# Comparisons that also sum, and a count taken as a difference

## The reference

```python
h = relu(layernorm(x))
msgs_f = mlp2([h[src], h[dst], edge_attr], W1_f, b1_f, W2_f, b2_f)     # 192 -> 128 -> 128
agg    = segment_sum(msgs_f, dst, 100000)
msgs_r = mlp2([h[dst], h[src], edge_attr], W1_r, b1_r, W2_r, b2_r)
agg   += segment_sum(msgs_r, src, 100000)
out = x + h + mlp2([agg, h], Wn1, bn1, Wn2, bn2)                        # 192 -> 128 -> 64
```

## Time and profile before

| what | us |
|---|---|
| median of 3 runs | 1618.86 (1618.42 to 1619.26) |
| the profiled execution | 1619.61 |
| its span | 1617.8 |
| GpSimd busy | 1111.7 |
| VectorE busy | 977.1 |
| scatters, L532, x392 | 633.4 |
| counts, L991, x392 | 168.8 |
| comparisons, L979, x392 | 144.8 |

### The profile page before, as it was taken

How to read it: one execution, slowest core, us unless ns; L and a number is a source line. 1 busy time by engine, 2 the same in 40 slices (tenths; PEclk the granted TensorE clock), 3 DMA queues, 4 the chain that set the end, 5 groups by cost and what they waited for, 6 DMA issues and landing times.

```text
span 1617.8 us, 29085 instructions
## 1 busy us (share of the span) xinstructions
PE 1288.9 (80%) x7070; PEld 978.6 (60%) x7070; DVE 977.1 (60%) x2902; ACT 946.8 (59%) x2256; POOL 1111.7 (69%) x1003
## 2 busy tenths in 40 slices
PE   5899998457777787778788887777777756899998
PEld 4777776245556565656566665555556644666665
DVE  7999999436666666666666666666666641222222
ACT  5888888345555555545555555555554524677776
POOL 7888888888888888888888888888888861000000
PEclk9999999768888877877877778788887877999999
DMA  6899998435555555555555555555555547999997
GB/s 214 293 317 314 313 313 284 130 58 108 109 108 109 108 103 103 104 102 104 103 103 100 100 102 102 102 102 101 103 104 103 100 72 228 355 352 352 344 344 274
DMA packets 238374, 280.71 MB, mean 174 GB/s; under 512 B 53170, under 2 KB 155200, under 8 KB 238348
## 3 DMA queue, kind: packets, MB, share of 16 engines
q1 hardware_dynamic: 168408, 241.57, 45.0%
q0 software_dynamic: 68992, 38.59, 20.6%
q10 hardware_dynamic: 948, 0.30, 0.1%
HBM read 162.62 MB, written 117.72 MB: 173 GB/s over the span
## 4 chain that ended last, share of the span: by engine, by line
POOL 33%; issue 22%; DMA 15%; PE 4%; DVE 4%; ACT 1%; POOLq 0%; SPq 0%; another core or an unknown queue 0%; DVEq 0%; ACTq 0%
POOL table L532 27%; DMA out_x<-ncentred 12%; POOL got_odd L514 6%; DMA table<-to_send,scatter_at 2%; DVE ncentred L1137 2%; DVE same L979 1%; DMA same<-table 1%; PE bank L820 1%; PE bank L833 1%; PE bank L871 1%; PE bank L818 1%; PE bank L846 1%; PE bank L882 0%; SPq L391 0%; ACT nh L639 0%
## 5 line engine op out<-in xcount | busy, mean ns | idle before, releaser
L532 POOL DMA_INDIRECT table<-to_send,scatter_at x392 | 633.4, 1616 | 133.7 <-issue 119.2
L846 PEld LDWEIGHTS bank<-message,same 128*128 128x128 f32 x1960 | 271.1, 223 | 42.1 <-issue 39.2
L846 PE MATMUL bank<-message,same 128*128 128x128 f32 x1960 | 292.1, 314 | 2.7 <-DVE message L1010 2.7
L639 ACT ACTIVATE nh<-nx,all_sums,all_rstd 128x64 f32<-128x64 f32 x784 | 280.1, 433 | 0.0
L514 POOL DMA_INDIRECT got_even<-in_x,gather_first x196 | 212.0, 1082 | 40.4 <-issue 35.1
L775 PE MATMUL bank<-wn_h,nturned 128*128 128x256 f32 x784 | 197.4, 396 | 30.2 <-ACT nhidden L683 21.8
L514 POOL DMA_INDIRECT got_odd<-in_x,gather_at x180 | 179.9, 999 | 54.8 <-issue 54.2
L804 PE MATMUL bank<-ident,h_ends 128*128 128x128 f32 x196 | 54.1, 371 | 203.2 <-DVE h_ends L1019 200.8
L1004 DVE TENSOR_TENSOR scatter_at<-moved,ids 128x4 int32<-128x4 f32 x98 | 16.1, 165 | 303.3 <-DMA table<-to_send,scatter_at 303.3
L818 PE MATMUL bank<-turned,w_ends 128*128 128x256 f32 x392 | 167.0, 516 | 36.5 <-ACT turned_edge L609 36.5
L775 PEld LDWEIGHTS bank<-wn_h,nturned 128*128 128x128 f32 x784 | 143.7, 193 | 66.4 <-issue 37.8
(11 more groups left out here) (78 smaller groups left out, 1917.6 us busy)
## 6 DMA issues: line engine op xcount, KB each, us to landing
nx<-in_x SPq DMA_DIRECT2D x194, 256.0 KB
table<-nhidden SPq DMA_DIRECT2D x97, 512.0 KB
same<-table SPq DMA_DIRECT2D x97, 512.0 KB, 5.4
others<-numbers SPq DMA_DIRECT2D x196, 128.0 KB
out_x<-ncentred SPq DMA_DIRECT2D x97, 256.0 KB, 4.2
nx<-out_x SPq DMA_DIRECT2D x55, 256.0 KB, 4.7
out_x<-nh SPq DMA_DIRECT2D x31, 256.0 KB
table<-to_send,scatter_at POOLq DMA_INDIRECT x392
```

The costliest lines, as they stand in the source:

```text
L532: pool.indirect_dma_start(table, bass.IndirectOffsetOnAxis(ap=scatter_at[s][:, k:k + 1], axis=0), to_send[s][:, k, :], None, compute_op=AL ...
L639: last = act.activation(nh[s][:, g, :], nx[place][:, g, :], ACT.Relu, bias=all_sums[:, at, g:g + 1].rearrange("p a g -> p (a g)"), scale=a ...
L846: last = pe.matmul(bank[6 + s][:, k * M:(k + 1) * M], same[s][:, o, k * P:(k + 1) * P], message[s][:, o, :], start=(o == k), stop=(o == KB ...
```

## The change

The comparisons of L979 get a second operation, an addition, and an output `matches` with one number per partition: the sum of the results over all their columns, that is all ends of the same node in tiles 0 to o. The count of L991 reads only the end's own tile of `same` (128 columns each), with a mask `from_here` that is 1 from the end itself on, multiplies by -1 and starts from `matches`. What is left are the equal ends in front. The mask shrinks from 512 to 128 columns, and the scratch output `junk` too. No instruction changes its place on any engine; in the code after it, VectorE's lines stand one further down, and L991 keeps its number.

```diff
--- before.py
+++ after.py
@@ -129,7 +129,7 @@
 
 
         ident = sb("ident", [P, P])
-        earlier = sb("earlier", [P, KB * P])
+        from_here = sb("from_here", [P, P])
         spare = sb("spare", [P, KB])
         eps = sb("eps", [P, 1])
         w1_ends = sb("w1_ends", [P, 2, M])
@@ -175,7 +175,8 @@
         hidden = two("hidden", [2, JT * P])
         message = two("message", [KB, M])
         same = two("same", [KB, KB * P])
-        junk = two("junk", [KB, KB * P], mybir.dt.bfloat16)
+        junk = two("junk", [KB, P], mybir.dt.bfloat16)
+        matches = two("matches", [KB])
         before = two("before", [KB])
         to_spare = two("to_spare", [KB])
         moved = two("moved", [KB])
@@ -501,13 +502,12 @@
             pool.iota(spare[:, :], pattern=[[P, KB]], base=SPARE, channel_multiplier=1,
                       allow_small_or_imprecise_dtypes=True).then_inc(s_const, 1)
             pool.memset(ident[:, :], 0.0).then_inc(s_filled, 1)
-            pool.memset(earlier[:, :], 1.0).then_inc(s_filled, 1)
+            pool.memset(from_here[:, :], 1.0).then_inc(s_filled, 1)
             pool.wait_ge(s_filled, 2)
             pool.affine_select(out=ident[:, :], in_=ident[:, :], compare_op=ALU.not_equal, fill=1.0, base=0,
                                pattern=[[-1, P]], channel_multiplier=1).then_inc(s_const, 1)
-            tail = earlier[:, (KB - 1) * P:]
-            pool.affine_select(out=tail, in_=tail, compare_op=ALU.is_gt, fill=0.0, base=0,
-                               pattern=[[-1, P]], channel_multiplier=1).then_inc(s_const, 1)
+            pool.affine_select(out=from_here[:, :], in_=from_here[:, :], compare_op=ALU.is_ge, fill=0.0, base=0,
+                               pattern=[[1, P]], channel_multiplier=-1).then_inc(s_const, 1)
 
             def gather(to, numbers, landed, tiles=range(KB)):
                 for k in tiles:
@@ -976,7 +976,8 @@
                 row = others[s][:, :, :, :].rearrange("p j e q -> p (j e q)")
                 for o in range(KB):
                     w = (o + 1) * P
-                    last = dve.tensor_scalar(same[s][:, o, 0:w], row[:, 0:w], ids[s][:, o:o + 1], None, ALU.is_equal)
+                    last = dve.tensor_scalar(same[s][:, o, 0:w], row[:, 0:w], ids[s][:, o:o + 1], None, ALU.is_equal,
+                                             ALU.add, accum_out=matches[s][:, o:o + 1])
                 last.then_inc(s_same[s], 1)
 
             def variance(i, s):
@@ -987,9 +988,9 @@
 
                 dve.wait_ge(s_same[s], i + 1)
                 for k in range(KB):
-                    w = (k + 1) * P
-                    last = dve.tensor_tensor_reduce(junk[s][:, k, 0:w], same[s][:, k, 0:w], earlier[:, KB * P - w:],
-                                                    1.0, 0.0, ALU.mult, ALU.add, before[s][:, k:k + 1])
+                    last = dve.tensor_tensor_reduce(junk[s][:, k, :], same[s][:, k, k * P:(k + 1) * P], from_here[:, :],
+                                                    -1.0, matches[s][:, k:k + 1], ALU.mult, ALU.add,
+                                                    before[s][:, k:k + 1])
                 last.then_inc(s_before[s], 1)
                 dve.tensor_tensor(to_spare[s][:, :], spare[:, :], ids[s][:, :], ALU.subtract).then_inc(s_tospare[s], 1)
                 dve.wait_ge(s_before[s], i + 1)
```

## The result

The changed kernel takes 1610.4 us (median of 6 runs, 1608.65 to 1614.83) against 1619.06 (6 runs, 1618.42 to 1621.99): ratio 0.994, 95% interval 0.9929 to 0.9951. It is 9 us faster, where +2.5 was forecast; the profiled execution took 1610.51 us where 1622.1 was forecast.

A forecast was written before the change was run, and what follows sets the result against it. GpSimd's gathers and scatters were taken as the bound; first scatters giving back about 14 us and thirds taking about 19 made +3.8, taken as +2.5: 1622.1 us profiled, 1621.4 beside the median, range 1610 to 1626.

The forecast's parts named there:

- The bound, and the mechanism: GpSimd bounds; scatters starting during a two-input VectorE instruction begin late by about its rest less 0.10 or 0.13 us.
- I take 1.65, since the row of the same kind of output has it: L979: four summing comparisons priced at 1.65 us like the old counts, +0.17 us per batch on VectorE.
- the two more small operands I take at nothing, at most 0.01 us each: L991: the shortened counts' added operands priced at nothing; four counts go from 1.65 to 0.84 us.
- the sensitivity: Forecast change by added price: 0.01 us more per comparison +2.5 us, 0.015 -1, 0.03 -7; 0.01 on comparisons and counts -3.
- rival 1: Sum L1048 slips behind the third scatter's start if prices are 0.03 us or more higher: -7 to -9 us, 1611; chance 0.24.
- The same working: New durations put into 90 full batches' starts: scatter excess 0.297 us a batch against 0.256 before, +3.8 us.
- There is no reason left for the first scatter to suffer: 0: First scatter beside L979: excess falls from 0.152 us to 0, giving back about 14 us over the stage.
- is the most the change can give: All 392 scatters: VectorE's instructions cost GpSimd (1.616 - 1.552) x 392 = 25 us, the largest possible gain.
- The second scatter: Second scatter, beside L1019: mean excess over 1.553 us forecast at 0.07, against 0.078 before.
- Rival 2: L979 comparisons keep their two-column rate, first two scatters stay, L1048 ends 0.8 us earlier: -2 us, 1617; chance 0.12.
- Rival 3: Nearly all batches meet the L1048 collision at the third scatter, some also pay at the second: +9 us, 1628; chance 0.13.
- Rival 4: Two-input instructions cost scatters nothing, only two-column ones do: -14 us, 1605; chance 0.03.

The follow-up runs named there:

- counts-alone kernel: Kernel before with only the counts cut to 128 columns, start value constant 1, plain comparisons, all rows to the spare rows: 1617.87 us, ratio 0.9991.
- The kernel with the sum sooner: Changed kernel with the count's last two small instructions put behind the sum nodes + h, which starts sooner: 1633.94 us, ratio 1.0083.
- as-priced kernel: Changed kernel with comparisons against a constant, counts started from a constant, matches left out, all rows to the spare rows: 1630.67 us, ratio 1.0061.
- the control: Kernel before with counts started at 1, so every row goes to the spare rows: 1619.37 us, ratio 0.9999.

## Why the prediction was wrong

**The bound, and the mechanism: right.** GpSimd bounds the stage, VectorE's own time does not count (0.8 us a batch less is worth nothing in the counts-alone kernel), and a scatter pays for a two-input instruction that is running when it starts. The kernel with the sum sooner was forecast to 25 us by that rule alone. In the ten traces it holds for all 213 scatters that started well inside the sum.

**The step that failed** is "I take 1.65, since the row of the same kind of output has it", with "the two more small operands I take at nothing, at most 0.01 us each". I matched the comparison to the count by its output and passed over its operand: the comparison takes the node numbers as a column in SBUF, the old count took constants. That column costs 0.06 us in every instruction: 346 against 286 ns for a summing comparison, 346 against 287 for a count. In four comparisons and four counts this is 0.47 us, and the sum starts that much later, behind the third scatter instead of over it. It was there to be read in the earlier trace rows: the free comparison took 0.47 us where 512 columns, two at a time, and the fixed 0.15 of a count make 0.42. I used the 0.47 to tell the rate and let the 0.05 left over go. (No run has the comparison without a sum against a constant, so that the 0.05 is the same cost is likely, not shown.) The count, newly given a column by the diff, then got the same nothing.

**How much hung on it.** The prediction did carry the sensitivity: -7 us for 0.03 more per comparison, and rival 1 for that case, at 1611. It was given 0.24, because the price I took was treated as known to 0.01 us when its row was of another form. That 1610.4 were measured beside its 1611 is luck: its working took 0.03 us and a first scatter that costs nothing. The same working with the measured 0.055 and 0.061 us leaves next to no excess, about -23 us (an estimate from the trace of the kernel before).

**The first scatter: half right.** 0.152 was to go to 0. It went to 0.083. With the summing comparison in its place, the collision with the plain one (0.07 us in the mean, 6 us over the stage) is gone: where the first comparison begins 0.07 to 0.29 us into the first scatter, as at 709.93 in the earlier trace rows and at 706.64 above, the scatter takes 1.75 us in each of 49 batches before and 1.63 to 1.64 in each of 47 after. But 0.08 us stay in every kernel. "There is no reason left for the first scatter to suffer: 0" had taken the 1.55 us of a scatter behind a scatter as the floor; of the 1.75 against 1.55 in the prediction 0.12 us are the collision and 0.08 are not. Of the 92 first scatters behind a gather none is under 1.627 us in any of the ten traces, also where VectorE is idle at the start; of the last five batches, which have no gathers, four take 1.55 (the fifth starts while L963, with two inputs, is running). So the 0.08 belong to the change from gathers to scatters, not to VectorE. In the changed kernel, a first scatter behind two gathers, and one of the last batches:

```profile
1278.08 1.63 POOL L532 DMA_INDIRECT table<-to_send,scatter_at  x1 [0.30 <-issue]
...
1297.50 0.48 DVE L979 TENSOR_SCALAR_CACHE_REDUCE same<-others,ids 128x256 f32<-128x256 int32 x1
1297.74 1.55 POOL L532 DMA_INDIRECT table<-to_send,scatter_at  x1 [2.57 <-DMA table<-to_send,scatter_at]
```

1.63 against 1.55, both with a summing comparison running. The sentence that 25 us "is the most the change can give" had some 7 us in it that no edit on VectorE could reach. It also hid how dear the forecast's own schedule is: the as-priced kernel has 0.370 us a batch where the working had 0.297, the 0.081 of the first scatter being the difference. (0.370 - 0.266) x 92 = 10 us over the control, and 11 were measured, not the +2.5 forecast. Both errors count: with the price of the column alone mended the working gives about -23 us, too low; with the 0.083 of the first scatter as well it gives 0.157 us a batch, about -9, which is the result (both are estimates).

**The second scatter** gained what I had not counted as a gain: 0.078 to 0.030, since L1020 (L1019 before) now starts behind it or at most 0.05 us ahead. By terms: (0.069 + 0.048 - 0.005) x 92 = 10 us, of which 9 are in the span.

**The rivals.** Rival 1 is what happened; its place is shown, its size is luck, as said. Rival 2 (two columns kept) falls by the 742 ns. Rival 3, the slower side, is what the as-priced and the sum-sooner kernels show, 11 us above the control and 12.5 above the kernel before. Rival 4 (two-input instructions cost nothing) falls by the 2.08 us above; the Trainium skill's inference in "SBUF — State Buffer", section "Who interferes with whom", that tensor_tensor does not stall descriptor generation, is not borne out here. The same section's rule, that the form of tensor_scalar that writes its accumulator leaves GpSimd alone, is borne out: 1.63 us beside one, against 1.75 beside the plain form in the same place. (The 1.55 us of the last batch above says nothing on it: the kernel before has 1.55 there too, beside plain comparisons.)

**VectorE's wait** ahead of the landing was to grow by 0.7 us a batch and fell, from 303.3 us in 95 waits to 252.2 in 92. Of the 0.64 us priced as saved, 0.47 went to the columns; the comparisons had taken 1.41 us in the mean before and not the 1.48 of one batch; the batch is 0.11 us shorter; the wait ahead of the bias sum (L1010, now L1011) for TensorE rose from 18.7 to 51.8 us; and 17.9 us of waiting now stand ahead of the variance (L985).

## What to carry to other kernels

Before pricing an instruction by a row of another, compare the operands too: a scalar taken from a column in SBUF cost 0.06 us here, in an instruction of 0.29 us. Take an instruction's floor from the same place in the order too: the scatter behind a gather had another. Where two engines collide only if one starts while the other is running, the busy time is not the measure; write down the starts of both, and if the margin is smaller than what the prices are known to, forecast both sides and say so with the chances. Then a reordering is a cheaper tool than a rewrite: the place of a single sum was worth 25 us.

## What the runs showed of the hardware

- A compare with a sum of 128 to 512 columns takes 346 to 742 ns, 1.03 ns a column; without the sum it took 0.47 us for 512 where nothing held it. The accumulator's read (83 ns) costs no time of its own: the next instruction starts with it.
- A per-partition scalar in SBUF in place of a constant adds 0.06 us to a compare with a sum (681 to 742) and to the custom multiply-and-sum (287 to 346).
- An indirect scatter takes 1.55 us on GpSimd behind another, 1.63 behind a gather; 1.75 behind a gather when a plain compare begins 0.07 to 0.29 us into it, 1.63 when it is a compare with a sum.
- A scatter that starts inside a VectorE instruction with two SBUF inputs is longer by the rest of that instruction less 0.11 to 0.13 us (all 213 starts inside the 512-column sum, in ten traces) or less 0.08 to 0.13 (182 inside the 256-column L1020). Those began 0.045 us or more ahead. Of 70 that began less than 0.035 us ahead none made the scatter over 0.04 us longer; between the two, 8 of 33 did.
